# Attention layers with small heads: scores by query for the maximum, then by key with the maximum as extra contraction rows

## The reference

```
scores = jnp.einsum('bkgld,bksd->bkgls', q, k) * scale
scores = scores + encoder_attention_mask[:, :, None, :, :]
attn = jax.nn.softmax(scores, axis=-1)
out = jnp.einsum('bkgls,bksd->bkgld', attn, v)
```

## Time and profile before

| | us |
|---|---|
| median of 3 runs | 1459.5 (1459.3 to 1462.95) |
| the profiled execution, its own time | 1460.95 |
| its span, first to last instruction | 1459.6 |
| first to last score of L1 | 744.9 to 851.9 |
| of L2 | 957.7 to 1141.6 |
| of L3 | 1248.2 to 1434.7 |

### The profile page before, as it was taken

The page is one execution under the profiler, slowest core; times in us unless marked ns, Lnnn a source line. Parts: engine busy times, 40 slices in busy tenths (PEclk is TensorE's granted clock), DMA queues, the critical chain, the costliest instruction groups (busy, mean ns, idle before and its releaser), DMA issues.

```text
span 1459.6 us, 27778 instructions
## 1 busy us (share of the span) xinstructions
PE 1261.7 (86%) x10205; PEld 1113.4 (76%) x10205; DVE 1015.3 (70%) x2544; ACT 855.0 (59%) x2071; POOL 432.1 (30%) x704
## 2 busy tenths in 40 slices
PE   7999999999999999997868869669999695688875
PEld 6999999999999999996756648546665384566553
DVE  6966667688756666786458865357787662698884
ACT  4856666677655656672147742157777431687773
POOL 3544545455534444442122211111110110111111
PEclk9999999999999999998969979879999897899997
DMA  5320000033100000140053300432440103321200
GB/s 164 106 59 1 2 1 5 1 95 110 30 2 1 2 1 2 30 116 5 10 81 54 45 4 1 82 62 47 59 66 1 33 22 57 54 37 36 43 2 15
DMA packets 52839, 56.23 MB, mean 39 GB/s; under 512 B 5408, under 2 KB 39520, under 8 KB 52704
## 3 DMA queue, kind: packets, MB, share of 16 engines
q1 hardware_dynamic: 52704, 54.46, 18.3%
HBM read 31.64 MB, written 1.05 MB: 22 GB/s over the span
## 4 chain that ended last, share of the span: by engine, by line
PE 67%; DVE 13%; ACT 7%; issue 5%; DMA 3%; SPq 2%; POOL 2%; DVEq 0%; ACTq 0%; POOLq 0%
PE bank L114 17%; PE bank L115 17%; PE bank L116 17%; PE bank L1283 5%; ACT E L1365 4%; PE bank L367 4%; PE bank L1252 3%; PE bank L1267 3%; DVE PT L1534 2%; DVE nm L1518 2%; DMA Q<-qP 2%; DVE Em L1524 2%; PE bank L167 1%; SPq L1130 1%; PE bank L1298 1%
## 5 line engine op out<-in xcount | busy, mean ns | idle before, releaser
L716 POOL TENSOR_SCALAR E<-E,rl 128x256 f32<-128x256 f32 x256 | 237.5, 939 | 0.0
L1252 PE MATMUL bank<-K,Q 72*128 72x256 bf16 (+2 forms) x512 | 121.9, 311 | 91.9 <-ACT E L1365 43.9
L1267 PE MATMUL bank<-ident,E 128*128 128x128 f32 x1280 | 187.0, 277 | 6.7 <-DVE PT L1534 4.1
L466 ACT ACTIVATE QTh<-bank,bqs 128x256 fp32r<-128x256 f32 x128 | 60.7, 474 | 183.1 <-PE bank L116 183.1
L1267 PEld LDWEIGHTS bank<-ident,E 128*128 128x128 f32 x1280 | 148.9, 142 | 24.5 <-DVE PT L1534 12.5
L1365 ACT ACTIVATE E<-bank,nm 128x256 f32<-128x256 f32 (+1 forms) x256 | 135.5, 584 | 53.1 <-DVE nm L1518 36.7
L1252 PEld LDWEIGHTS bank<-K,Q 97*128 97x128 bf16 (+1 forms) x512 | 39.1, 99 | 148.9 <-ACT E L1365 92.4
L1534 DVE COPY PT<-bank 128x512 f32<-128x512 f32 x181 | 123.7, 684 | 33.4 <-PE bank L1267 33.1
L1365 ACT ACTIVATE E<-Em,nm 128x256 f32<-128x256 f32 x256 | 113.8, 501 | 47.7 <-DVE nm L1524 47.6
L714 POOL TENSOR_TENSOR pb<-E,rl 128x2 f32<-128x2 f32 x128 | 33.0, 258 | 332.0 <-DVE rl L594 332.0
L1524 DVE CUSTOM_DVE_ANT_0 Em<-bank,M 128x256 f32<-128x256 f32 x256 | 96.2, 418 | 45.6 <-PE bank L1252 45.2
(11 more groups left out here) (458 smaller groups left out, 4291.6 us busy)
## 6 DMA issues: line engine op xcount, KB each, us to landing
stage<-in_wts SPq DMA_DIRECT2D x99, 256.0 KB, 3.0
Q<-qP SPq DMA_DIRECT2D x84, 128.0 KB
K<-kP SPq DMA_DIRECT2D x48, 128.0 KB
K<-qP SPq DMA_DIRECT2D x24, 128.0 KB
K<-kP SPq DMA_DIRECT2D x36, 32.0 KB
X<-in_x SPq DMA_DIRECT2D x4, 256.0 KB, 6.2
stage<-in_ctx SPq DMA_DIRECT2D x4, 256.0 KB, 3.4
M<-in_mask SPq DMA_DIRECT2D x4, 256.0 KB, 3.1
```

The costliest lines, as they stand in the source:

```text
L716: m = pool.tensor_scalar(s.E[:, i % 3, t, 0:256], s.E[:, i % 3, t, 0:256], s.rl[:, r, t:t + 1], None, ALU.mult)
L1252: z = pe.matmul(ps[:, o:o + s.NK], s.Q[0:s.R, j, h, t * 128:t * 128 + 128], s.K[0:s.R, j, h // s.rep, :], start=True, stop=True)
L1267: z = pe.transpose(bank[:, k * 256 + t * 128:k * 256 + t * 128 + 128], s.E[:, i % (LAG + 1), t, o:o + 128], c.ident[:])
```

## The change

L1, L2 and L3 form each head's scores twice. The first time, as before, with queries as rows, and only the maximum is taken; the exponential there is gone. The negated maxima of a group of G heads (4, 2, 4) are split in three bf16 parts by POOL (`maxima_parts`), transposed in one go by PE (`turn_maxima`, into a free part of the attend's bank), copied by ScalarE, and sent by one DMA on SP to three further contraction rows of Q (`maxima_rows`), 6G rows of 256 bytes. K has rows of ones there, set by DMA at the start of the layer. D steps after its first scores (10, 6, 10) the head's scores are formed again with keys as rows and the maxima included (`weights_by_key`), two matmuls of 256 columns for each 256 keys, and one exponential of 128x512 writes PT directly. E, its transposes and the copies to PT are gone. A score bank is free when its maximum is taken.

In L3 the mask by query and key is added to the second scores by two matmuls of a float32r identity with the transposed mask (loaded as mask3t, split in two parts by VectorE). Q, K and V have three slots in L1 and L3 and two in L2, where the preparations start two and five steps later than before. The last steps of a batch follow D + 1 steps behind, and the four weight pieces loaded in L2 are issued behind the first batch's preparations.

```diff
+GROUP = {1: 4, 2: 2, 3: 4}
+DELAY = {1: 10, 2: 6, 3: 10}
+RING = {1: 3, 2: 2, 3: 3}
+
+TILE_COUNTS = {"s": (64, 128, 128), "mx": (64, 128, 256), "st": (64, 128, 128), "ex": (64, 128, 128),
+               "pv": (16, 16, 32), "os": (16, 16, 32), "g": (16, 32, 32)}
...
-        self.Q, self.K = sb("Q", [128, 2, nh, 256], BF16), sb("K", [128, 2, nkv, NK], BF16)
-        self.V = sb("V", [128, 2, nkt, nkv, 32])
+        self.Q, self.K = sb("Q", [128, self.NR, nh, 256], BF16), sb("K", [128, self.NR, nkv, NK], BF16)
+        self.V = sb("V", [128, self.NR, nkt, nkv, 32])
...
-        self.NPT = 5 if l == 2 else 6
         self.hTh, self.hTl = sb("hTh", [128, 2, 256], F32R), sb("hTl", [128, 2, 256], F32R)
-        self.E = sb("E", [128, LAG + 1, 2, NK])
+        self.NPT = 6
         self.PT = sb("PT", [128, self.NPT, nkt, 256])
-        self.nm = sb("nm", [128, 4, 2])
+        self.nm = sb("nm", [128, 4, self.G, 2])
+        self.nr = sb("nr", [128, 2, self.G, 2])
+        self.np = sb("np", [128, 2, 3, self.G, 2], BF16)
+        self.rows = sb("rows", [128, 2, 128], BF16)
...
+            self.M3, self.MT = sb("M3", [128, 2, 2, 256]), sb("MT", [128, 2, 2, 256])
+            self.MTh, self.MTl = sb("MTh", [128, 2, 512], F32R), sb("MTl", [128, 2, 512], F32R)
+            self.Em = sb("Em", [128, 4, 256], BF16)
+            self.identR = sb("identR", [128, 128], F32R)
...
+        self.SB, self.STB, self.OB, self.PB, self.MB = c.B[0:2], c.B[2:4], c.B[4], c.B[5:7], c.B[7]
+        self.RB = self.OB[0:6 * self.G, 256:320].bitcast(BF16)
...
+        k_steps = ["k0", "k0F", "k00", "k012", "v0", "v0F"]
+        m_steps = ["mask", "maskrow"] if l != 3 else ["mask"] + [None] * 13 + ["maskparts"]
+        self.chains = {1: ((0, m_steps), (0, q_steps), (0, k_steps)), 2: ((0, m_steps), (2, q_steps), (5, k_steps)),
+                       3: ((0, m_steps), (0, q_steps), (0, k_steps))}[l]
...
-        b, k = (i - 3) // self.nh - 1, (i - 3) % self.nh
+        b, k = (i - self.D - 1) // self.nh - 1, (i - self.D - 1) % self.nh
...
+    def turns_at(self, i):
+
+        return [(i - 2) // self.G] if (i - 2) % self.G == self.G - 1 and 0 < i - 1 <= self.N else []
+
+    def attends_at(self, i):
+
+        v = i - self.D - 1
+        return [v // 4] if 0 <= v < self.N and v % 4 == 3 else []
...
-            w.wait_ge(S["t_s"], s.o["s"] + (b - 1) * s.nh * (2 if l == 2 else 1))
+    for j in range(s.NR):
+        for r in range(s.R, s.R + 3):
+            sp.dma_start(s.K[r:r + 1, j, :, :], c.units[0:s.nkv * s.NK // 256, :]).then_inc(S["ld_ones"], 16)
+
+    def ring_free(b):
+
+        if b >= s.NR:
+            w.wait_ge(S["t_st"], s.o["st"] + (b - s.NR + 1) * s.nh * s.units)
...
+    def maxima_rows(g):
+
+        b, h = g * s.G // s.nh, g * s.G % s.nh
+        w.wait_ge(S["t_rows"], s.o["g"] + g + 1)
+        sp.dma_start(s.Q[s.R:s.R + 3, b % s.NR, h:h + s.G, :], s.rows[0:6 * s.G, g % 2, :]
+                     ).then_inc(S[f"dma_rows{g % 2}"], 16)
...
-                w.wait_ge(S["t_ex"], s.o["ex"] + 2 * (i - 1) + t + 1)
+                w.wait_ge(S["t_mx"], s.o["mx"] + 2 * (i - 1) + t + 1)
...
-    def turn(i):
-        w.wait_ge(S["t_ex"], s.o["ex"] + 2 * i + 2)
-        for u in range(nkt // 2):
-            n = i * (nkt // 2) + u
-            bank = s.PTB[n % 2]
-            w.wait_ge(S["t_evA"], s.o["evA"] + s.evacs(n - 1, "A"))
-            w.wait_ge(S["t_evD"], s.o["evD"] + s.evacs(n - 1, "D"))
-            for t in range(2):
-                for k in range(2):
-                    o = (2 * u + k) * 128
-                    z = pe.transpose(bank[:, k * 256 + t * 128:k * 256 + t * 128 + 128],
-                                     s.E[:, i % (LAG + 1), t, o:o + 128], c.ident[:])
-            z.then_inc(S["t_T"])
-
-    def attend(gi):
-        b, g, j = gi // (nh // 4), gi % (nh // 4), gi // (nh // 4) % 2
+    def turn_maxima(i, g):
+        w.wait_ge(S["t_np"], s.o["g"] + g + 1)
+        w.wait_ge(S["t_os"], s.o["os"] + s.attended_before(i + 1))
+        w.wait_ge(S["t_rows"], s.o["g"] + g)
+        w.wait_ge(S["ident_b"], 1)
+        pe.transpose(s.RB, s.np[:, g % 2].rearrange("p a h t -> p (a h t)"), c.ident_b[:]).then_inc(S["t_rT"])
+
+    def weights_by_key(i):
+
+        b, h, r = i // nh, i % nh, i // nh % s.NR
+        g = i // s.G
+        w.wait_ge(S[f"dma_rows{g % 2}"], 16 * ((s.o["g"] + g) // 2 + 1))
+        w.wait_ge(S["ld_ones"], 16 * ONES[l])
+        for u in range(s.units):
+            n = i * s.units + u
+            bank = s.STB[n % 2]
+            w.wait_ge(S["t_ex"], s.o["ex"] + n - 1)
+            for k in range(2):
+                o = (2 * u + k) * 128
+                z = pe.matmul(bank[:, k * 256:k * 256 + 256], s.K[0:s.R + 3, r, h // s.rep, o:o + 128],
+                              s.Q[0:s.R + 3, r, h, :], start=l != 3 or k == 0, stop=l != 3, skip_group_check=l == 3)
+            if l == 3:
+
+                w.wait_ge(S["mask_low"], b + 1)
+                pe.matmul(bank[:], s.identR[:], s.MTh[:, b % 2, :], start=False, stop=False, skip_group_check=True)
+                z = pe.matmul(bank[:], s.identR[:], s.MTl[:, b % 2, :], start=False, stop=True, skip_group_check=True)
+            z.then_inc(S["t_st"])
+
+    def attend(i, gi):
...
+        w.wait_ge(S["t_ex"], s.o["ex"] + (i0 + 4) * s.units)
         w.wait_ge(S["t_os"], s.o["os"] + gi)
+        w.wait_ge(S["t_rows"], s.o["g"] + s.turned_before(i))
...
+    for i in range(s.iterations()):
+        if i < s.N:
+            scores(i)
+        if 0 <= i - s.D < s.N:
+            weights_by_key(i - s.D)
+        for gi in s.attends_at(i):
+            attend(i, gi)
+        for g in s.turns_at(i):
+            turn_maxima(i, g)
+        for b, x in s.preps(i):
+            prep(b, x)
+        for b, x in s.posts(i):
+            post(b, x)
...
-        r = i % 4
-        w.wait_ge(S["t_T"], s.o["T"] + (i - LAG) * (s.nkt // 2))
-        for t in range(2):
-            w.wait_ge(S["t_mx"], s.o["mx"] + (i + 1 if l == 1 else 2 * i + t + 1))
-            if l == 3:
-                src = s.Em[:, i % 3, t, :]
-            elif l == 2:
-                src = s.SB[t][:]
-            else:
-                src = s.SB[i % 2][:, t * 256:t * 256 + 256]
-            act.activation(s.E[:, i % (LAG + 1), t, :], src, ACT.Exp, bias=s.nm[:, r, t:t + 1],
-                           scale=-1.0 if l == 3 else 1.0).then_inc(S["t_ex"])
-
-    def turned(i):
-        for u in range(s.nkt // 2):
-            n = i * (s.nkt // 2) + u
-            if EVAC[l][n % len(EVAC[l])] == "A":
-                w.wait_ge(S["t_T"], s.o["T"] + n + 1)
-                w.wait_ge(S["t_pv"], s.o["pv"] + (i - s.NPT) // 4 + 1)
-                act.copy(s.PT[:, i % s.NPT, 2 * u:2 * u + 2, :], s.PTB[n % 2][:].rearrange("p (a b) -> p a b", a=2)
-                         ).then_inc(S["t_evA"])
+        for u in range(s.units):
+            n = i * s.units + u
+            w.wait_ge(S["t_st"], s.o["st"] + n + 1)
+            w.wait_ge(S["t_pv"], s.o["pv"] + (i - s.NPT) // 4 + 1)
+            act.activation(s.PT[:, i % s.NPT, 2 * u:2 * u + 2, :].rearrange("p a b -> p (a b)"), s.STB[n % 2][:],
+                           ACT.Exp).then_inc(S["t_ex"])
...
+    def maxima_rows(g):
+        w.wait_ge(S["t_rT"], s.o["g"] + g + 1)
+        if g >= 2:
+            w.wait_ge(S[f"dma_rows{g % 2}"], 16 * ((s.o["g"] + g) // 2))
+        act.copy(s.rows[0:6 * s.G, g % 2, :], s.RB).then_inc(S["t_rows"])
...
+        elif x == "maskparts":
+            w.wait_ge(S[f"ld_mt{j}"], 16 * (b // 2 + 1))
+            if b >= 2:
+                w.wait_ge(S["t_st"], s.o["st"] + (b - 1) * nh)
+            raw = s.MT[:, j].rearrange("p a b -> p (a b)")
+            dve.tensor_scalar(s.MTh[:, j, :], raw, BIG, None, ALU.max).then_inc(S["mask_high"])
+            w.wait_ge(S["mask_high"], b + 1)
+            dve.scalar_tensor_tensor(out=s.MTl[:, j, :], in0=raw, scalar=BIG, in1=f32(s.MTh[:, j, :]), op0=ALU.max,
+                                     op1=ALU.subtract).then_inc(S["mask_low"])
...
+    def maxima_parts(g):
+
+        n, nm, nr, np = s.o["g"] + g + 1, s.nm[:, g % 4], s.nr[:, g % 2], s.np[:, g % 2]
+        w.wait_ge(S["t_mx"], s.o["mx"] + (g + 1) * s.G * (1 if l == 1 else 2))
+        w.wait_ge(S["t_rT"], n - 2)
+        pool.tensor_copy(np[:, 0], nm).then_inc(S["t_np0"])
+        w.wait_ge(S["t_np0"], n)
+        pool.tensor_tensor(nr, nm, np[:, 0], ALU.subtract).then_inc(S["t_nr"])
+        w.wait_ge(S["t_nr"], n)
+        pool.tensor_copy(np[:, 1], nr).then_inc(S["t_np1"])
+        w.wait_ge(S["t_np1"], n)
+        pool.tensor_tensor(np[:, 2], nr, np[:, 1], ALU.subtract).then_inc(S["t_np"])
+
...
+    m3t = np.ascontiguousarray(A["mask_Bx1xSxS2_ff0"][:, 0].transpose(0, 2, 1))
```

More of the change, by code:

```diff
@@ L1044, in prep @@
     def prep(self, k):
-        return [x[k] for x in (self.m_steps, self.q_steps, self.k_steps) if k < len(x)]
+        return [x[k - o] for o, x in self.chains if 0 <= k - o < len(x) and x[k - o]]
     def preps(self, i):
```

(54 more changed lines are left out.)

200 lines of the change are left out of this document (81 added, 119 removed).

## The result

Forecast 1451.5 us, range 1418 to 1487, faster. Measured 1547.7 us (median of four runs) against 1459.4: ratio 1.061, 95% interval 1.058 to 1.063. It is slower, and 60.7 us above the upper end of the range. The profiled execution has a span of 1546.1 us against 1459.6.

The account below looks back on a forecast made before the run. No engine was full (TensorE busy 86%), so waits counted. L1 -10, L2 -23 and L3 +25 gave -8 us on 1460.95, so 1453; the runs' median lies 1.45 lower, so 1451.5 us, range 1418 to 1487.

Parts of the forecast that it names:

- +3 us for POOL's queue: L1: the maxima's parts come behind the 1.16 us splits on POOL, +3 us; no wait for the rows.
- 2 us a batch: L2: rows due 11.8 us after spreads needing 12 us, and parts waiting on POOL, cost 2 us a batch, +6 us.
- the coupling factor: Batch period over the largest engine's time: 1.15 in L1 (bounds 1.0, 1.25), 1.17 in L2 (bounds 1.05, 1.25).
- The third case: Rival, no change: the factor stays at 1.19 in L1 and 1.22 in L2, giving 1461 us; chance 0.12.
- the rows behind the spread in L3: L3: maxima rows' DMAs wait behind Q's spreads; 22 us for three, 6.5 us for clock, together +28 us, bounds 0 and 45.
- rows not held: Rival: the rows don't wait behind the spread in L3, so 28 us fall away, giving 1423 us; chance 0.13.
- L3 without that wait: L3's batches apart from the rows' wait: TensorE becomes the bound, inner batches 46.3 us, sum -14 us, bounds -25 and 0.
- the clock only in three places of L3: After each of three pauses in L3 TensorE runs 4.3 us at half speed, 2.2 us lost each time, 6.5 us.
- starts 6, 3, 6: Layer starts: added DMAs of ones and shifted loads delay first scores by 6, 3 and 6 us; sum +15 (5 to 20).
- Tails 5: Layer ends: last score to first post step grows from 5.1 to 10.1 us in L1; +5 in each layer, +15 (8 to 22).
- The slower case: Rival: the rows' wait decides in L2 (+12) and L1 (+9) too, L3 +10 more; sum +23, 1475 us; chance 0.33.
- three signs of being wrong: Rows land within 3 us during a spread; L2's batches stay above 43 us; mask matmuls cost over 0.5 us a head.

Follow-up runs that it names:

- the change of queue: The changed kernel with the DMA of the maxima rows in L3 issued on ScalarE's queue instead of SP's: 1545.5 us, ratio 1.060.
- the run with four slots: The changed kernel with maxima split by VectorE, L3's second scores eighteen steps behind the first, and four slots for the rows instead of two: 1502.9 us, ratio 1.030.
- The pair with and without mask matmuls: The changed kernel with maxima split by VectorE, eighteen steps in L3 and four row slots: 1502.9 us; the same without L3's two mask matmuls per head: 1494.5 us.
- VectorE's split: The changed kernel with the four small operations that split a group's maxima issued by VectorE instead of POOL: 1536.4 us, ratio 1.052.
- two kernels that differ in L1 only: The changed kernel with all that helped together, 1476.2 us, and the same with L1's second scores eight steps behind the first instead of ten, 1489.6 us.

## Why the prediction was wrong

- **Failed: "+3 us for POOL's queue" in L1 and "2 us a batch" in L2.** The parts were priced by their length and by the one 1.16 us operation ahead. They stand behind up to four, and those behind ScalarE; TensorE, in whose order the transpose stands, waited 26.9 and 17.4 us. Taking POOL's work away in either direction brings L1's scores from 115.5 to 101.1 or 100.3, half of L1's miss of 29.5. In L2 it gives 15 us when VectorE takes the operand parts and 1 when it takes the maxima.
- **Failed: the coupling factor, 1.15 and 1.17 "over the largest engine".** With POOL out of the way L1's batch is 27.8 us at clock 1.00 with TensorE busy 21.5 (19.5 forecast): 1.29, above my bound of 1.25, and 1.43 times my count. In L2 the shortest inner batch of any run is 43.6; the batch of 44.4 above is 1.11 times a TensorE busy 40.1 at clock 0.92, but 1.38 times the 32.1 of my count, which is the yardstick of the prediction. The earlier trace rows had shown the sign: 43.0 busy against the 38.3 of my count for before. Which waits make up the rest of the factor was not tested. The third case (coupling eats the gain) was nearer than its chance of 0.12.
- **Right: the rows behind the spread in L3, +28.** Three waits of 27.6 us in all, where 22 were put down for them; taking them away is worth 32 us with what the clock does behind them. The rule of the Trainium skill (DMA: Bandwidth & Descriptors, "Why a DMA increments its semaphore by 16 and not by 1") put the rows on engines of the spread; that the change of queue leaves the landing at 11.5 to 13.5 us agrees with it. So do the semaphore's events: each DMA of the rows has four, as the one issued at 1354.10, with one after 1.25 us and three after 13.5, 13.6 and 13.8 us, which fits three data engines. Which three they are the trace doesn't tell. The case "rows not held" is refuted.
- **Failed: L3 without that wait.** I gave -14 us for the batches; measured in the run with four slots they are 49.4 and 49.9 against 46.3. The mask matmuls cost 0.55 us a head (1315.35 to 1315.90 below) instead of 0.46, 2.9 us a batch. VectorE, put at 28 us, is busy 32.4 in the batch after. The rest, and the last batch's 45.2 instead of 40, I didn't resolve.

```profile
1315.35 0.47 PE L1289 MATMUL bank<-MTh,identR 128*128 128x512 f32 x1
1315.67 0.40 PE L1290 MATMUL bank<-MTl,identR 128*128 128x512 f32 x1
1315.90 0.39 PE L1260 MATMUL bank<-K,Q 72*128 72x256 bf16 x2
```

- **Failed: the clock only in three places of L3, 2.2 us each.** The waits in L1 and L2 did it too (0.85 and 0.89 over a batch, 1.00 in all three of the earlier trace rows), and a pause of L3 is followed by a stretch at 0.54. L3's first batch, which was to be 6 us shorter for want of second scores, ran at 0.74, and at 0.61 where those were put off further. The pair with and without mask matmuls shows the same from the other side: a TensorE with less to do can get the slower clock.
- **Right: starts 6, 3, 6** (6.4, 3.6, 6.1), though L2's 3 was right for the wrong reason. Tails 5 came at 6.3 to 7.6.
- **The slower case** had the right side but the wrong carrier: it added the rows' wait to L1 and L2, where as the change stands no row comes late (the longest landing 6.7 us, 0.2 us of waits). What it describes does come once POOL is out of the way: with VectorE's split TensorE waits 8.7 us for the rows in L2. Its 1475 is 73 us short. Its terms don't add up to it either: 12, 9 and 10 are 31, which on 1451.5 gives 1482.5; the +23 is the distance from the kernel before.
- **Of the three signs of being wrong** that I had named, two came: L2's batches stayed above 43 us (48.6), and the mask matmuls cost more than 0.5 us a head (0.55).

## What to carry to other kernels

A small operation put on a lightly loaded engine can cost the whole queue ahead of it, and what that queue waits for: before moving a link of TensorE's loop to POOL, read POOL's waits, not its busy share. Work taken from TensorE is worth little where it isn't what sets the pace (17 and 8 of 70 us here), and may cost clock. Try such a scheme layer by layer: here one of three layers gains, once POOL's order is mended.

## What was not expected of the hardware

- A DMA of 6 KB on a second queue, issued at once, landed after 11.5 to 13.5 us beside nine of 128 KB; 1.9 us is the median.
- TensorE at half clock, 9.87 of 10 us busy, after a stretch of 2.36 of 5; the same batch with the mask matmuls in it stayed at 1.00. L3's first batch, with second scores for only part of its heads, ran at 0.61 to 0.74, where before the change it had 0.95.
- The small operations on the maxima take 0.17 us on VectorE and 0.19 to 0.20 on POOL, where I took 0.26.
- The same code of L2 took 226 and 234 us in two kernels that differ in L1 only, at clocks of 0.89 and 0.86 over its scores.
